# A two-layer macaron transformer kernel: softmax sums on 128 partitions by 32, the layer norm's root beside its fine sum, and a new written-out order

## The reference

```
x = x + 0.5 * ffn0(layernorm(x))    # int-quantised weights (w-128)*scale, silu(gate)*up, hidden size 704
x = x + attn0(layernorm(x))         # 16 heads of 16, rotary positions, causal softmax
x = x + 0.5 * ffn0(layernorm(x))
x = x + 0.5 * ffn1(layernorm(x))    # ternary weights round(w/mean|w|), sigmoid(x1)*x2
x = x + attn1(layernorm(x))         # 16 query heads, 4 key heads, ALiBi bias, causal softmax, bias bo
x = x + 0.5 * ffn1(layernorm(x))
```

## Time and profile before

| what | us |
|---|---|
| median of 3 runs | 561.21 |
| the profiled execution, its own time | 562.23 |
| its span, first to last instruction | 560.5 |
| TensorE (PE) busy | 538.5 |
| VectorE (DVE) busy | 460.0 |
| ScalarE (ACT) busy | 401.3 |
| GpSimd (POOL) busy | 340.2 |

### The profile page before, as it was taken

The page is one execution under the profiler, slowest core; times in us unless marked ns, Lnnn a source line. Parts: engine busy times, 40 slices in busy tenths (PEclk is TensorE's granted clock), DMA queues, the critical chain, the costliest instruction groups (busy, mean ns, idle before and its releaser), DMA issues.

```text
span 560.5 us, 12972 instructions
## 1 busy us (share of the span) xinstructions
PE 538.5 (96%) x5060; PEld 305.4 (54%) x5060; DVE 460.0 (82%) x813; ACT 401.3 (72%) x605; POOL 340.2 (61%) x427
## 2 busy tenths in 40 slices
...
DMA packets 20525, 31.76 MB, mean 57 GB/s; under 512 B 7360, under 2 KB 8768, under 8 KB 20312
## 3 DMA queue, kind: packets, MB, share of 16 engines
q1 hardware_dynamic: 20464, 30.94, 16.0%
...
## 4 chain that ended last, share of the span: by engine, by line
PE 60%; DVE 11%; POOL 10%; ACT 6%; issue 6%; DMA 4%; SPq 2%; DVEq 0%; POOLq 0%; ACTq 0%
PE PS L593 18%; PE PS L617 10%; PE PS L704 8%; PE PS L669 5%; PE PS L684 5%; PE PS L635 4%; PE PS L719 3%; PE PS L577 3%; DVE MX L1058 3%; DMA CH<-wd 3%; ACT PB L846 2%; PE PS L541 2%; DVE ST L871 1%; POOL PB L1162 1%; PE PS L651 1%
## 5 line engine op out<-in xcount | busy, mean ns | idle before, releaser
L846 ACT ACTIVATE PB<-PS 128x1024 f32<-128x1024 f32 x160 | 158.2, 1024 | 39.7 <-PE PS L684 37.8
L1058 DVE TENSOR_REDUCE MX<-PS 128x2 f16<-128x1024 f32 (+2 forms) x192 | 158.1, 865 | 18.3 <-PE PS L541 17.9
L593 PE MATMUL PS<-XT,WGU 128*128 128x512 f16 x660 | 157.4, 381 | 2.6 <-DVE MX L1058 0.7
L1134 POOL TENSOR_TENSOR HH<-TH,HH 128x512 f16<-128x512 f32 x71 | 82.7, 1173 | 86.7 <-ACT HH L814 86.3
L593 PEld LDWEIGHTS PS<-XT,WGU 128*128 128x128 f16 x660 | 60.0, 98 | 74.4 <-issue 5.4
L1162 POOL TENSOR_SCALAR_AFFINE_SELECT PB<-PB 128x512 f32<-128x512 f32 (+1 forms) x140 | 73.3, 551 | 43.2 <-ACT PB L846 43.1
L617 PE MATMUL PS<-WD,HH 128*128 128x256 f16 x660 | 77.7, 273 | 0.8 <-POOL HH L1134 0.6
L704 PE MATMUL PS<-PB,V 128*32 128x512 f32 (+3 forms) x1024 | 75.3, 435 | 1.1 <-POOL PB L1162 0.7
L617 PEld LDWEIGHTS PS<-WD,HH 128*128 128x128 f16 x660 | 62.8, 98 | 13.1 <-issue 2.2
L814 ACT ACTIVATE HH<-TH 128x512 f16<-128x512 f32 (+1 forms) x86 | 53.5, 627 | 14.4 <-DVE TH L1004 6.5
L669 PE MATMUL PS<-SK,SQ 63*128 63x256 f16 (+3 forms) x512 | 59.7, 300 | 3.6 <-ACT PB L846 0.9
...
## 6 DMA issues: line engine op xcount, KB each, us to landing
...
RB<-scratch SPq DMA_DIRECT2D x64, 64.0 KB, 2.3
...
SQ<-MT SPq DMA_DIRECT2D x128, 1.0 KB
...
```

What stands on the lines that cost most here:

```text
L593: m = e.matmul(o[:, :], WGU[l][:, k, col:col + P], rows_of(f)[j][:, k, :], start=j == 0 and k == 0, stop=j == 1 and k == 1)
L846: e.activation(PB[Q % 2][:, j, :, :], two_banks("s", i), ACT.Exp, scale=0.25).then_inc(a_exp, 1)
L1058: e.tensor_reduce(mx[:, :, pr, t], o[:, :, col:col + (t + 1) * P], AX.X, ALU.max, negate=True).then_inc(a_max, 1)
L1134: e.tensor_tensor(hh[1][:, s * T:(s + 1) * T], value_of(j)[0], hh[0][:, s * T:(s + 1) * T], ALU.subtract).then_inc(f_lo, 1)
```

## The change

Four things are changed.

1. DC is a tile of 128 partitions by 2 by 32 instead of 128 by 64. The sums of a half lie on 128 partitions, 32 each. The two DMAs move rows of 128 bytes to and from 128 partitions, where they moved rows of 256 bytes on 64.
2. In a fine layer norm bn_aggr comes before the two sums on VectorE. GpSimd's r waits for bn_aggr alone, does VE and YR, and only then waits for the fine sum and does OFF.
3. The first unit of all is treated as the last: ScalarE normalises tiles 0 and 1, VectorE (step X) tiles 2 and 3. The second half of the gate and up weights is converted by VectorE (new step g), and no longer by ScalarE; counts of p_act go down by one for it.
4. All order strings and the banks are new. The numbers of steps of each kind on each engine are the same, but for the X and g of part 3 (TensorE has 17 z before and after).

```diff
+BOTH = (0, NF - 1)
...
     "pe":
-        "zzzzzzzzzttzggGgGggtGgGtGzzazdddgdggGtzGGggatguuzGGqqvgdqdgddGgggqGvGGuugGtqqtzmmmmgmzmmgqmqmsdsmGsd"
+        "zzzzzzzttzgGgggGGgGtzztgzGzagGgddddggGztzzgzGtGuugGaqqvgddgdvdqgGgqgtGGGguuGtqqqzmmmgmmgqmmdmmGsdsms"
...
-        DC = sb("DC", [P, 64])
+        DC = sb("DC", [P, 2, 32])
...
             if Q == 0:
-                w.wait_ge(p_act, 3)
+                w.wait_ge(p_act, 2)
+                w.wait_ge(p_gu, 1)
...
-            if f == NF - 1 and t >= 2:
-                w.wait_ge(f_xd, t - 1)
+            if f in BOTH and t >= 2:
+                w.wait_ge(f_xd, 2 * BOTH.index(f) + t - 1)
             else:
-                w.wait_ge(f_xn, NT * f + t + 1)
+                w.wait_ge(f_xn, NT * f + t + 1 - (2 if f else 0))
...
-                    e.dma_start(DC[64 * u:64 * u + 64, :],
-                                OT[1:P:32, 2 * u:2 * u + 2, :].rearrange("a g (s t) -> a (g s) t", t=64)
+                    e.dma_start(DC[:, u, :],
+                                OT[1:P:32, 2 * u:2 * u + 2, :].rearrange("a g (s t) -> a (g s) t", t=32)
...
-                    e.dma_start(scratch[n % 2, u], DC[64 * u:64 * u + 64, :]).then_inc(t_so[u], 16)
+                    e.dma_start(scratch[n % 2, u].rearrange("r (h t) -> (r h) t", h=2), DC[:, u, :]).then_inc(t_so[u], 16)
...
-                    if i < 2:
-                        w.wait_ge(l_gu[i], 16)
-                        e.activation(WGU[0][:, i, :], rgui[:, i, :], ACT.Copy, bias=-128.0).then_inc(p_act, 1)
+                    if i == 0:
+                        w.wait_ge(l_gu[0], 16)
+                        e.activation(WGU[0][:, 0, :], rgui[:, 0, :], ACT.Copy, bias=-128.0).then_inc(p_act, 1)
...
-                    for t in range(2 if i == NF - 1 else NT):
+                    for t in range(2 if i in BOTH else NT):
...
-                if fine:
-                    e.tensor_reduce(FM[:, 0:64], xv.rearrange("p t (a c) -> p (t a) c", c=16), AX.X, ALU.add).then_inc(ln, 1)
                 for t in range(NT):
                     w.wait_ge(ln, base + t + 1)
                     e.bn_aggr(MV[z][:, t, :], ST6[z][:, t, :]).then_inc(ln, 1)
                 if fine:
-                    w.wait_ge(ln, base + NT + 1)
+                    e.tensor_reduce(FM[:, 0:64], xv.rearrange("p t (a c) -> p (t a) c", c=16), AX.X, ALU.add).then_inc(ln, 1)
+                    w.wait_ge(ln, base + 2 * NT + 1)
...
+                elif c == "g":
+                    w.wait_ge(l_gu[1], 16)
+                    e.tensor_scalar(WGU[0][:, 1, :], rgui[:, 1, :], -128.0, None, ALU.add).then_inc(p_gu, 1)
...
-                    dc = DC[64 * (i % 2):64 * (i % 2) + 64, :]
-                    e.reciprocal(dc, dc).then_inc(t_rc, 1)
+                    e.reciprocal(DC[:, i % 2, :], DC[:, i % 2, :]).then_inc(t_rc, 1)
...
-                    w.wait_ge(f_ln, LNF0[i + 1])
+                    w.wait_ge(f_ln, LNF0[i] + 2 * NT)
...
-                    if l == 0:
-                        e.tensor_scalar(OFF[0][:, :], FM[:, 64:68], -1.0 / D, None, ALU.mult).then_inc(f_mean, 1)
-                    else:
+                    if l == 1:
                         e.tensor_scalar(OFF[0][:, :], MV[0][:, :, 0], -1.0, None, ALU.mult).then_inc(f_mean, 1)
                     w.wait_ge(f_ve, i + 1)
                     e.tensor_tensor(YR[0][:, :], VE[0][:, :], HALF[:, :], ALU.pow).then_inc(f_rt, 1)
+                    if l == 0:
+                        w.wait_ge(f_ln, LNF0[i + 1])
+                        e.tensor_scalar(OFF[0][:, :], FM[:, 64:68], -1.0 / D, None, ALU.mult).then_inc(f_mean, 1)
```

More of the change, by code:

```diff
@@ new lines @@
+        "msdsmgmmsdsmmpmssgmsGsGsmspsmsgmmGmpsmssmsgmmsGmmpsmsvmsvsmsmuummpqssqosmoomssoddsmqqmspttmsdgggsGdG"
+        "smgmmspmsGmsmgsgsmGGmpmsvsmsddmsvumsdudqqsspmmoottoosmsggqsgmmgGgsGGsmpmsgmssqGttGpsssddssgddGgpmmgg"
+        "gGGmmmvgvmGuuGoooommsqsmqsmmqdmsdsmmddsmsmssmmspmmsmttsspsmgGggGGssmggGgGsmmpmtdtddssdsmggmspsmmgvGg"
+        "uugGsmqqgGsmsqGGoommspsmdddmsdmssoosmmmpmttsssgggmsGGsspmmgsmgGsmGGsmgsmpmsmvmddmssdsmsdmsspmsttooos"
+        "mmogguuGgGsqmmsqgqGsmgGgGmmspsmsdsmsdmmsddsmpmsmsmsmpsttvmsggGgsmsGgGgGgGsmtmmsddtddsmppmsouooougmsm"
@@ new lines @@
+        "qsgqssqgssGGsspmsmgmGmmpmmmvgGmsgsmsGsmsttmmpssgdsmmdddoooosmsgGgmmsGmmpssgssGggssspssGGttpgGggddddG"
+        "ggGgGGooooddddttgggGgGGgGGgdddd",
+    "dve":
+        "NXgwttNhhkhhNhtwwwtwhwhwdwwdwhnhNtwhkwuuhthpqwpqwdwdpnhqpqhhkhuuhhqpttqpmmmsmhmsxmmmpmqdmpxmhqmmmsmx"
+        "mdmkmshhmnmxmmsmhmmxcmsmmmhmcmxmmmuumpqpqmxomoNdmppmqtqtcmshsxhsdhmkmmsmhmmxsmshmhmnmcdxmmuudNqpqpmm"
+        "ottomxNhmmhpqhkmhmmxhphqttcsdhdnskhmmcsshhmmmsmxhsuuohommmlmmxllmdmmdmmxNmmmmmtxtNmhchhkmhhhmmxmtdtd"
+        "mnmsshmkmchsusuhmlslshxmhhlommmxdmdmNmmmomttxNhhhcmkmmmxhmhmmhmmcxmdmmdmnmttomxomsuhsushhmlkmlslmhxs"
+        "hsmhmmmdmcxmdmNmmmxmNttmhchmkhhhhmmxmtddntmmuooumhmxcllklhNhmmmmmxhmmmmhcmhxmmmttmmdhdxooNmhmmhmmxkh"
+        "cththchhdkhhhhooNdXdttdhkhhhhhdd",
@@ new lines @@
+    "act":
+        "wXxxTwttthtXhhthxxhtwwhtthwXthwtxwthYyyxthkhhkkvwQttQXtktvkhtYQyytQhhhxxkkkhhtwTQteQeeeeteewQQhoeete"
+        "eheehoeethoeeeetehYoeevheveecyyoceeeeeQQeXeoxxeQtQttehehtheoeetetehhhoecveeYevyeyeceXoxxeettQQetXhhe"
+        "ehttoeteehhxxhoeeeQQteethohttthchYtvvcyyhehQeQeQeeeeeeeoXexxeeoettthhheteththXhoexxeeetetcoehYtvytyh"
+        "ehQtQtceheQhheeeoeeeXoxxeeettetehehohteteehhtehoeXvceeeeeecoxxeYetytyhteQhehQtQtethhehoeeeeeeoeeeXoe"
+        "xxevttXthhetheththehexcexocYeyoytehQeQeetQteeeheoehtXovteteeeehhhxxeeoectcheettehXhoeeeteteeeeehxxot"
+        "ohhttchtthhchtthhXxxthttthhthhth",
@@ new lines @@
+        "6135026305320372054613046136741041657013650462063526016406430642063751630517342350235126302673021403"
+        "0642403604214626402406240625051370513157402175130643750273107624205460260325617450621430641376064202"
+        "5436116351361064526045602745275103651365203705346134724064202407136570146342176043416056314064725042"
+        "0570242054205264026046345160435063257607506341601253750264276240735631041654025603502365036525027025"
+        "40264502720452062120537203610413463042672046032503464315275046357372145632576341240",
@@ L247, in macaron_kernel @@
         l_ali = [sem(f"l_ali{z}") for z in range(2)]
-        p_act, p_pool, p_dve, p_pe, p_set, p_tab, p_sc = (sem(f"p_{n}") for n in ("act", "pool", "dve", "pe", "set", "tab", "sc"))
+        p_act, p_pool, p_dve, p_pe, p_set, p_tab, p_sc, p_gu = (sem(f"p_{n}") for n in ("act", "pool", "dve", "pe", "set", "tab", "sc", "gu"))
         f_ln, f_ve, f_mean, f_rt, f_off, f_xn, f_xd = (sem(f"f_{n}") for n in ("ln", "ve", "mean", "rt", "off", "xn", "xd"))
@@ L583, in tensor_program @@
                     if l == 0:
-                        w.wait_ge(p_act, 2)
+                        w.wait_ge(p_act, 1)
+                        w.wait_ge(p_gu, 1)
                     else:
```

58 lines of the change are left out of this document (17 added, 41 removed).

## The result

The changed kernel takes 552.34 us (median of 4 runs, 552.14 to 553.68) against 560.94 (4 runs, 560.22 to 562.04): ratio 0.9855 [0.9842, 0.9869], which is 8.1 us less (8.6 by the two medians). The forecast of 559.6 and its range down to 556.8 are both missed: the change brings five times what was predicted. The profiled execution spans 550.4 us, 10.1 less than the one of before. That one lay 1.3 us above its median, so about 9 of the 10 are the change.

A forecast was written before the change was run, and what follows sets the result against it. VectorE was taken to bound the front to some 120 us, TensorE the rest. From the profiled 562.23 us, 0.7 (start), 0.1 (reciprocals) and 0.8 (order) gave 560.6, or 559.6 for the median; range 556.8 to 563.4.

The forecast's parts named there:

- What bounds the kernel: VectorE to some 120 us, with 5.3 us of waits; TensorE from there, 8.1 us to win at most.
- The root and the split: At the start: OFF 1.1 us earlier, hi parts 2.2, counted as 0.7 us won; bounds 1.1 lost, 2.2 won.
- I take them at nothing: Four later fine norms: 1.0 to 1.2 us shorter from residual to transposes, under other TensorE work, so nothing won.
- The reciprocals: Sixteen, 0.547 to 0.3 us each; sums to output projection between 0.28 us shorter and 0.4 longer; 0.1 won.
- All of it behind 120 us, where it has 56 us free: nothing: VectorE's 4 us saved by shorter reciprocals lies in its free time behind 120 us and wins nothing.
- it matters only in the last halves: The changed way from sums to output projection counts only where little work is left to hide it: 0.1 us won.
- The order: New strings on all five queues: 0.8 us won in front; bounds 5.3 us won and as much lost.
- I take a third of these 2.5 us, 0.8: Front: VectorE's later waits for TensorE (1.5 us) and ScalarE's gates (1.0) shrink by a third.
- for the stretch from 120 us I take nothing: Behind 120 us: no gain or loss from the order, with up to 8.1 us there to win.
- The head start: Rival at the start: table load delays the first gate to 15.3 us or beyond, start's gain lost; 561.0 us, chance 0.2.
- The new order fits much better: Rival: wins most of VectorE's 5.3 us of waits and something of TensorE's 8.1; 557.2 us, chance 0.18.
- The clock didn't fall at the first scores: Rival claimed more 1.2 GHz stretches there, a filler being gone: 563.8 us; chance 0.2, shared with a worse-fitting order.

The follow-up runs named there:

- e1_hand: Changed kernel with the order strings of the kernel before, so reciprocals, root and split first unit without the new order: 560.03 us, ratio 0.9995.
- a2_root_behind: Changed kernel with the root put behind the fine sum again, as before: 554.75 us, ratio 0.9896.
- b1_no_fillers: Changed kernel without the nine filler steps (72 matmuls) between the first gate and the end of the first scores: 555.41 us, ratio 0.9906.
- e2_order: Kernel before with the new order strings alone: 558.46 us, ratio 0.9959.
- a4_table_first: Changed kernel with Silu's table loaded ahead of everything, as before: 553.27 us, ratio 0.9876.
- a1: Changed kernel with reciprocals of 64x64 and DMA rows of 256 bytes, as before: 554.32 us, ratio 0.9890.
- a3: Changed kernel without the split of the first unit; ScalarE does both weight conversions and all four tiles: 555.93 us, ratio 0.9908.
- a5: Changed kernel without the split of the first unit and with Silu's table loaded ahead of everything: 555.93 us, ratio 0.9908.
- b7: Changed kernel with the new order up to some 500 us and the order of before from there on: 554.86 us, ratio 0.9899.

## Why the prediction was wrong

**What bounds the kernel.** Right: VectorE in front, TensorE behind, and the room was read right, 5.3 us of VectorE's waits in front and 8.1 us of TensorE's behind 120. The gains lie inside these bounds: 4.0 of 5.3, and 4.9 behind 106 us.

**The root and the split.** Right in mechanism and nearly in size at the start. OFF at 8.46 + 0.20 = 8.66 (forecast 8.8), normalising from 8.70 (9.1), hi parts from 10.43 (10.5), VectorE's conversion 0.89 us (1.1), first gate 14.31 (14.6), first product 15.33 (15.7). The term was 0.7, the lead at the first product is 0.76. What the forecast of the hi parts leaves out is the row of fillers ahead of the transposes: with the old 72 they would have begun at 12.0, as e1_hand shows. Whether "I take them at nothing" for the later fine norms was wrong is open; a2_root_behind has a second loss behind 121 us, but so has b1_no_fillers, where the root stays. Wrong was to take the lead at the first product as the worth of these parts; under the new order each is worth 2.3 to 3.0 us.

**The reciprocals.** The duration was right (0.344 for 0.3). "All of it behind 120 us, where it has 56 us free: nothing" and "it matters only in the last halves" are wrong: the new layout is worth 1.2 to 2.0 us under the new order. The DMA was bounded on the wrong side, between nothing and 0.2 us longer; the write lands 0.4 us sooner, so these two steps alone make a half's way 0.6 shorter, and not 0.28 at most. VectorE's free time says that its work fits, not that no one waits for what comes of it.

**The order.** This is the failed step: a term of 0.8 us for the new strings, added to the others as if it didn't depend on them. "I take a third of these 2.5 us, 0.8": measured 4.0 of VectorE's waits in front, and "for the stretch from 120 us I take nothing": the lead grows by 4.9 behind 106 us (of 9.9 in two profiles that lie 1.5 us further apart than the medians). The bound in front was right and the value in it wrong. A row of waits by name (2.5 us) had been used for the whole, though the windows gave 5.3; and a new written-out order of every engine was taken as neighbours swapped at random, when it fits the new durations, as the row of fillers shows. e1_hand and e2_order show that this is the term: each by itself gives what I forecast for the whole in size (0.3 to 1.1 and 2.3, against 1.6), both together 8.1. My sum had no term that exists only when both are there.

**The rivals.** The head start is not lost on ScalarE: a4_table_first shows that the table load costs nothing. By the rule that I cited from the Trainium skill's page "ScalarE: Activation LUTs", section "What ACT_TABLE_LOAD costs", a drain of 1.38 us would stand with this load too; the trace shows 1.29 us from its start to the next activation, and the measurement decides. "The new order fits much better" had the right mechanism, with a chance of 0.18, and the wrong size: I let it win 1 us of TensorE's 8.1. The clock didn't fall at the first scores, nor anywhere in the changed kernel's four executions; where it fell in a kernel near this one (a1, a2, a3, a4, a5, b7), the time was 1 to 3.4 us above the same kernel's at the full clock. The range's lower end, 556.8, came from that rival's size, and so could not reach 552.

**What stays open.** Which swaps in the strings take up which shortened step. One is named at the start, the row of fillers, and the tail's term is bounded; why the halves of the order are worth 7.8 us together and 3.8 apart is not explained beyond the 1.8 us at one seam. The 3.3 us of lead between 106 and 500 us, of which TensorE's free time gives some 2.4, were not taken apart further.
